# Two graph layers on one core: the segment softmax taken per chunk and clipped by carries, its key exchange brought forward, more value tiles, and other engines for three steps

## The chip, the cores and the metric

The kernel runs on one core of one Trainium2 chip. The metric is the device time of one execution in microseconds (us). Three runs of the kernel before gave 3033.27, 3036.22 and 3034.06 us, a median of 3034.06 us.

## The reference

A graph has 3125 nodes of 256 features and 50,000 edges sorted by destination. Layer one is three hops of weighted neighbour sums, each with two 256x256 products; layer two is one step of graph attention with 8 heads. Each is added to its input and layer-normalised.

```python
# layer 1, per hop
Hn = segment_sum(H[cols] * vals, rows) @ Wn[i].T + bn[i];  H = Hn + H @ Ws[i].T + bs[i];  H = elu(H) (not last)
# layer 2
alpha = <h_src, a_src> + <h_dst, a_dst> + sum(relu(edge_attr @ edge_W.T + edge_b) * h_dst)      # per edge and head
alpha = where(alpha >= 0, alpha, 0.2 * alpha)
ex = exp(alpha - segment_max(alpha, dst)[dst])
out = segment_sum(h_src * ex / segment_sum(ex, dst)[dst], dst) + bias
x = layernorm(x + out)
```

## The kernel before, in words

Edges are sorted on the chip and laid out as 416 chunks of 128, so that a chunk touches one window of 128 destination nodes (25 windows are used). All synchronisation is written by hand: each engine has its own program, and each operation that another must wait for raises a named semaphore. The order on every engine is the order of the code.

The stages, with their lines:

1. **Sort**, to about 556 us: GpSimd (POOL) scatters records by indirect DMA (L579, L589, L604).
2. **Adjacency blocks**, 570 to 1100 us: 90 steps of U = 8 blocks. For each block VectorE (DVE) or ScalarE (ACT) builds one-hots of the source (`rhot`), ACT weighs one-hots of the destination (`lw`, L1084), TensorE (PE) multiplies them into PSUM (L826), DVE merges the block with the one before of the same place (L1549), and SyncE (SP) stores it (128 KB, L484), to an address that it loads from a table once per step (L478). `RA` says how many of a step's 8 `rhot` tiles DVE makes in one instruction (L1538); the others ACT makes as a Square (L1090) and a Relu (L1093). A merge waits for the store of the same slot one step earlier.
3. **Hops**, to 2125 us, bound by PE's products (L896). At the end PE turns the node features back (L917), ACT copies them to `hcur` (L1135), and the keys of the chunks are transposed (L927) and copied by ACT (L1154). DVE marks the key breaks in `brk3` (L1660 to L1664).
4. **Score**, 2138 to 2658 us: POOL gathers the rows of the source nodes, 4 chunks per group, 104 groups (L618); SP stores each group for later (L524); PE, ACT and DVE look up the destination rows and form alpha. For each block of 16 chunks alpha is transposed into `alT` (a lane holds one chunk and head, 128 edges along the row), and DVE scans it forward and backward for the segment maximum inside the chunk (`scan_chunks`, L1700 and L1702).
5. **Carries**, 2658 to 2730 us: POOL adds the bias to all of `hcur` (L622). DVE writes the maxima of the chunk ends and their keys to `ends` (L1730, L1731); they go through DRAM to 8 lanes of 416 elements, where DVE scans over the chunks (L1735 to L1768), and back through DRAM as `cin`, the maximum that enters a chunk from the left and from the right (SP at L537, L540, L543 and L546). DVE scans all 26 blocks again with `cin` as start, forward (L1772) and backward (L1777), and subtracts (L1782). ACT takes the exponential (L1200), PE transposes back, ACT stores it to `s_sb` (L1203).
6. **Attend**, 2733 to 2982 us, in groups of 4 chunks: SP loads the kept rows (L528), POOL multiplies them by the exponentials into `val`, a ring of 2 tiles (L636); ACT builds one-hots (L1209, L1215) and copies the exponentials themselves into columns 256 to 263 of `val` (L1227), PE multiplies (L1013), DVE adds each chunk's result to its window (L1789). Which window that is, DVE reads from a table into registers, 8 values at a time, with a TENSOR_LOAD (L400).
7. **End**, 2982 to 3034 us: DVE divides by the sums (L1823), POOL adds to `hcur` (L650), DVE takes the statistics (L1828, L1840), the square root is ACT's (L1236), DVE normalises all 25 windows (L1849), SP stores them (L552, L555).

## Time and profile before

| what | us |
|---|---|
| median of three runs | 3034.06 |
| profiled execution, its own time | 3035.49 |
| its span, first to last instruction | 3033.7 |
| TensorE busy in it | 2438.7 (80%) |
| GpSimd busy | 1880.7 (62%) |
| VectorE busy | 1702.3 (56%) |
| ScalarE busy | 993.5 (33%) |

The profiled execution took 1.4 us longer than the median, and 1.8 us of its time lie around the span. Of the chain of work that ended last 54% is on PE, 12% on POOL and 7% on DVE, with 11% in which an engine waited for nothing that shows. The busy shares are means over the seven stages, which have different bounds. Engine names ending in q (DVEq, SPq) are an engine's sequencer: register work and the issuing of DMAs, which count as no busy time.

### The profile page before, as it was taken

How to read it: one execution, taken by the hardware profiler on the slowest of the kernel's cores; microseconds unless marked ns; L12 is line 12 of the kernel's file. 1: busy time of each engine (PE TensorE's matmuls, PEld its weight loads, DVE VectorE, ACT ScalarE, POOL GpSimd, SP SyncE). 2: the span in 40 equal slices, each digit the busy share in tenths (PEclk: the TensorE clock that was granted, in tenths of full speed). 3: DMA queues.
4: the chain of work that ended last, by engine and by line, in shares of the span. 5: the costliest groups of instructions: out<-in, count | busy, mean ns of one | idle time of the engine just before them, and what ended most of it. 6: DMA issues, size and time to landing. Idle time of an engine off the chain costs nothing.

```text
span 3033.7 us, 46185 instructions
## 1 busy us (share of the span) xinstructions
PE 2438.7 (80%) x9398; PEld 1579.2 (52%) x9399; DVE 1702.3 (56%) x4008; ACT 993.5 (33%) x2944; POOL 1880.7 (62%) x1739
## 2 busy tenths in 40 slices
PE   6999976477777679999899999999777767708882
PEld 5888843255555544445444454445555555506661
DVE  7765559899999940001344301113677666675557
ACT  1222221377777720000000000000433333318882
POOL 4777777787777870000067777760777777737774
PEclk9999999699999999999999999998888888859996
DMA  4000010355555555443344444452677777737772
GB/s 128 3 4 3 3 25 3 115 184 183 183 183 182 183 184 154 134 132 110 100 125 122 118 128 129 136 145 72 187 217 219 219 218 218 207 65 218 228 228 83
DMA packets 425353, 415.42 MB, mean 137 GB/s; under 512 B 85090, under 2 KB 411193, under 8 KB 424633
## 3 DMA queue, kind: packets, MB, share of 16 engines
q1 hardware_dynamic: 367385, 348.28, 36.8%
q0 software_dynamic: 57888, 66.23, 9.7%
q8 instruction: 32, 0.52, 0.1%
q14 instruction: 48, 0.39, 0.0%
HBM read 247.08 MB, written 167.17 MB: 137 GB/s over the span
## 4 chain that ended last, share of the span: by engine, by line
PE 54%; POOL 12%; issue 11%; DVE 7%; DVEq 4%; DMA 4%; ACT 3%; SPq 3%; ACTq 1%; POOLq 0%
PE psum L896 27%; POOL gath L618 7%; PE psum L826 5%; PE psum L708 5%; POOL rows_by_pair L579 5%; PE psum L693 3%; DVEq L400 2%; ACT lw L1084 2%; PE psum L888 2%; PE psum L968 2%; DMA gath<-gat_rows,rec 2%; SPq L484 2%; PE psum L1013 1%; PE psum L767 1%; PE psum L684 1%
## 5 line engine op out<-in xcount | busy, mean ns | idle before, releaser
L604 POOL DMA_INDIRECT rows_by_dst<-rec,place x392 | 381.6, 974 | 512.8 <-DVE place L1441 385.1
L896 PE MATMUL psum<-a_t,acc 128*128 128x512 f32 (+1 forms) x1400 | 553.7, 551 | 0.0
L589 POOL DMA_INDIRECT rows_by_low_digit<-rec,place x392 | 459.8, 1173 | 128.0 <-issue 128.0
L618 POOL DMA_INDIRECT gath<-gat_rows,rec x416 | 401.4, 965 | 214.1 <-issue 115.5
L826 PE MATMUL psum<-rhot,lw 128*128 128x256 f32 x1440 | 371.1, 414 | 169.7 <-ACT lw L1084 143.0
L579 POOL DMA_INDIRECT rows_by_pair<-rec,place x392 | 385.3, 983 | 161.9 <-issue 126.8
L826 PEld LDWEIGHTS psum<-rhot,lw 128*128 128x128 f32 x1440 | 281.9, 205 | 258.9 <-ACT lw L1084 182.2
L896 PEld LDWEIGHTS psum<-a_t,acc 128*128 128x128 f32 x1400 | 257.3, 195 | 272.1 <-issue 268.3
L1549 DVE SCALAR_TENSOR_TENSOR merged<-merged,same_of,psum 128x256 f32<-128x256 f32 x720 | 298.2, 476 | 19.1 <-PE psum L826 17.0
L896 PE MATMUL psum<-a_t,x 128*128 128x512 f32 (+1 forms) x700 | 294.4, 549 | 0.0
L1084 ACT ACTIVATE lw<-lhot,recs_pair 128x128 f32<-128x128 bf16 x720 | 228.5, 388 | 178.2 <-DVE lhot L1532 138.2
L968 PE MATMUL psum<-x,acc 128*128 x832 | 260.4, 461 | 4.6 <-DVE acc L1678 4.4
L1013 PE MATMUL psum<-ht 128*128 128x264 f32 x832 | 203.7, 397 | 45.7 <-DVE acc L1789 39.2
L636 POOL TENSOR_TENSOR ht<-gath,digits 128x1024 f32<-128x1024 f32 x104 | 197.2, 1913 | 54.5 <-PE psum L1013 48.5
L708 PEld LDWEIGHTS psum<-table,ohhiT 32*128 32x128 f32 x784 | 181.1, 318 | 53.5 <-issue 32.0
L968 PEld LDWEIGHTS psum<-x,acc 128*128 128x128 f32 x832 | 181.6, 233 | 51.5 <-issue 17.2
L1678 DVE TENSOR_TENSOR acc<-wT,psum 128x528 f32<-128x528 f32 x208 | 145.3, 698 | 104.8 <-PE psum L968 76.2
L1013 PEld LDWEIGHTS psum<-ht 128*128 128x128 f32 x832 | 154.1, 192 | 95.1 <-DVE acc L1789 59.7
L708 PE MATMUL psum<-table,ohhiT 32*128 32x16 f32 x784 | 202.2, 375 | 1.7 <-ACT table L1044 1.7
L1625 DVE TENSOR_SCALAR et<-et 128x512 f32<-128x512 f32 (+1 forms) x28 | 11.0, 394 | 335.1 <-ACT et L1112 334.6
L896 PEld LDWEIGHTS psum<-a_t,x 128*128 128x128 f32 x700 | 126.2, 191 | 114.0 <-issue 109.0
L1319 DVE SCALAR_TENSOR_TENSOR terms<-psum,kst,earlier 128x128 f32<-128x128 f32 (+1 forms) x392 | 139.9, 412 | 44.8 <-PE psum L693 34.3
(311 smaller groups left out, 3301.9 us busy)
## 6 DMA issues: line engine op xcount, KB each, us to landing
a_t<-adjacency SPq DMA_DIRECT2D x450, 256.0 KB, 2.7
adjacency<-merged SPq DMA_DIRECT2D x721, 128.0 KB
gat_h_by_edge<-gath SPq DMA_DIRECT2D x104, 528.0 KB, 4.1
gath<-gat_h_by_edge SPq DMA_DIRECT2D x104, 528.0 KB, 4.1
gath<-gat_rows,rec POOLq DMA_INDIRECT x416
rows_by_pair<-rec,place POOLq DMA_INDIRECT x392
rows_by_low_digit<-rec,place POOLq DMA_INDIRECT x392
rows_by_dst<-rec,place POOLq DMA_INDIRECT x392
```

The source lines that it names most:

```text
L579: pool.indirect_dma_start(out=rows_pair, in_=rec[:, c, :], out_offset=bass.IndirectOffsetOnAxis(ap=place[:, 0, c:c + 1], axis=0), in_offse ...
L589: pool.indirect_dma_start(out=rows_low, in_=rec[:, c, :], out_offset=bass.IndirectOffsetOnAxis(ap=place[:, 1, c:c + 1], axis=0), in_offset ...
L604: pool.indirect_dma_start(out=rows_dst, in_=rec[:, c, :], out_offset=bass.IndirectOffsetOnAxis(ap=place[:, 0, c:c + 1], axis=0), in_offset ...
L618: pool.indirect_dma_start(out=gath[:, g % 4, c % 4, :], out_offset=None, in_=hh_dram, in_offset=bass.IndirectOffsetOnAxis(ap=rec_i[:, c, 0 ...
L636: nc.gpsimd.tensor_tensor(val[:, q % 2, :, 0:D].rearrange("p c (h d) -> p c h d", h=HEADS), gath[:, q, :, 0:HX].rearrange("p c (h d) -> p ...
L708: pe.matmul(bank[7 * s][:, j * LO:(j + 1) * LO], ohhiT[:, 4 * s + j, :], table[:, half, :], start=True, stop=True, skip_group_check=True). ...
L826: pe.matmul(bank[j % 4][:, 0:SW], lw[:, p, j, :], rhot[:, p, j, :], start=True, stop=True).then_inc(s_bmm, 1)
L896: i = pe.matmul(sums[b], table_g[:, w, b * P:(b + 1) * P], a_t[:, q % NA, 0:width(g)], start=False, stop=w == USED - 1)
L968: i = pe.matmul(bank[4 + j][:, 0:HX], ohT[:, q % 2, j * P:(j + 1) * P], x0[:, bass.ds(ws[4 * (q % 2) + j], 1), :].rearrange("p c k -> p (c ...
L1013: pe.matmul(bank[4 * (q % 2) + j][:, 0:HX], onehot[:, q // 2, 4 * (q % 2) + j, :], val[:, q % 2, j, :], start=True, stop=True).then_inc(s_ ...
L1084: nc.scalar.activation(lw[:, p, j, :], lhot[:, p, j, :], ACT.Copy, scale=recs_pair[:, bass.ds(at, 1), 2]).then_inc(s_lw, 1)
L1549: v.scalar_tensor_tensor(out=merged[:, j, :], in0=merged[:, (j - 2) % U, :], scalar=same_of[:, bass.ds(s, 1)], in1=bank[j % 4][:, 0:SW], o ...
```

## The change

* `RA` is 5, so of a step's 8 `rhot` tiles DVE makes 5 and ACT 3.
* At the end of the hops the keys are transposed first; then the features are turned back, and DVE adds the bias as it stores them to `hcur`. ACT's copies and POOL's addition are gone.
* `scan_chunks` has nine operations per block instead of two: both scans; a scan each that marks with 0 the lanes of the chunk's last and first segment (others are very low); copies of the chunk's end maxima to `ends`; and three subtractions. After the carries have come, two clipping passes per block (`lower_first`, `lower_last`) replace scan, scan and subtraction.
* The keys of the chunk ends have a DRAM exchange of their own: stored when the breaks are marked, ahead of SP's first kept group, and read behind its last. Of the carry computation what depends on keys alone stands ahead of the wait for the end maxima. SP exchanges the maxima ahead of its loads of the first four kept groups.
* `val` is a ring of 4 tiles, and POOL, DVE and ACT wait for an earlier product. DVE copies the exponentials into it, two groups ahead, and ACT's copies are gone.
* The end is written out window by window in three parts (`FINAL`: windows 0 to 8, 9 to 17, 18 to 24). Statistics and root of a part are taken as soon as its windows are there. ACT normalises the first two parts and three windows of the last, DVE four. Five stores take the place of four.
* Semaphores are merged, which moves nothing.

```diff
-RA = 6
+RA = 5
+FINAL = [(0, 9, 9), (9, 18, 18), (18, USED, 21)]
+LOCAL = 9
...
-        val = ht_t[:, 0:8 * HX].rearrange("p (s c d) -> p s c d", s=2, c=4)
+        val = ht_t[:, 0:16 * HX].rearrange("p (s c d) -> p s c d", s=4, c=4)
...
+            sp.wait_ge(s_brk, 5)
+            sp.dma_start(edge_key_dram, end_keys[:, :, :].rearrange("p b k -> p (b k)")).then_inc(s_ends, 16)
+            sp.wait_ge(s_ends, 16)
             for g in range(NQ):
...
-            nc.gpsimd.tensor_tensor(hcur[:, :, :], hcur[:, :, :], bias_b[:, :].unsqueeze(1).broadcast_to([P, USED, D]),
-                                    ALU.add).then_inc(s_bias, 1)
...
-                    if not (first and q < 2):
-                        pool.wait_ge(s_mm, 4 * (g - 1))
+                    if not first:
+                        pool.wait_ge(s_mm, 4 * (g - 3))
...
-            for w in range(USED):
-                act.wait_ge(s_xb, w + 1)
-                nc.scalar.copy(hcur[:, w, :], bank[w % 4][:, 0:D]).then_inc(s_x1, 1)
...
-                    nc.scalar.copy(val[:, q % 2, :, D:HX], s_sb[:, bass.ds(4 * g, 4), :]).then_inc(s_vx, 1)
...
+            for w in range(USED):
+                dve.wait_ge(s_xb, w + 1)
+                v.tensor_tensor(hcur[:, w, :], bank[w % 4][:, 0:D], bias_b[:, :], ALU.add).then_inc(s_x1, 1)
...
             def scan_chunks(b):
...
+                v.tensor_tensor_scan(row, stop[:, 0:P], a, -BIG, ALU.add, ALU.max).then_inc(s_loc, 1)
+                v.tensor_tensor_scan(in_last[:, ::-1], stop[:, 1:P + 1][:, ::-1], low, 0.0, ALU.add, ALU.max).then_inc(s_loc, 1)
+                dve.wait_ge(s_loc, n + 1)
                 v.tensor_tensor_scan(back[:, ::-1], stop[:, 1:P + 1][:, ::-1], row[:, ::-1], -BIG, ALU.add,
-                                     ALU.max).then_inc(s_bw, 1)
+                                     ALU.max).then_inc(s_loc, 1)
+                dve.wait_ge(s_loc, n + 3)
+                v.tensor_tensor_scan(row, stop[:, 0:P], low, 0.0, ALU.add, ALU.max).then_inc(s_loc, 1)
+                v.tensor_copy(ends[:, b, 0:1], back[:, P - 1:P]).then_inc(s_loc, 1)
+                v.tensor_copy(ends[:, b, 1:2], back[:, 0:1]).then_inc(s_loc, 1)
+                dve.wait_ge(s_loc, n + 6)
+                v.tensor_tensor(back, a, back, ALU.subtract).then_inc(s_loc, 1)
+                v.tensor_tensor(row, a, row, ALU.subtract).then_inc(s_loc, 1)
+                dve.wait_ge(s_loc, n + 8)
+                v.tensor_tensor(a, a, in_last, ALU.subtract).then_inc(s_loc, 1)
...
+            def lower_first(b):
+                v.scalar_tensor_tensor(out=dotT[:, b, :], in0=sdeT[:, b, :], scalar=cin[:, b, 0:1], in1=dotT[:, b, :],
+                                       op0=ALU.subtract, op1=ALU.min).then_inc(s_first, 1)
...
+            def lower_last(b):
+                dve.wait_ge(s_first, b + 1)
+                v.scalar_tensor_tensor(out=alT[:, b, :], in0=alT[:, b, :], scalar=cin[:, b, 1:2], in1=dotT[:, b, :],
+                                       op0=ALU.subtract, op1=ALU.min).then_inc(s_mx, 1)
...
+            def exp_columns(g, q, first):
+                if not first:
+                    dve.wait_ge(s_mm, 4 * (g - 3))
+                v.tensor_copy(val[:, q, :, D:HX], s_sb[:, bass.ds(4 * g, 4), :]).then_inc(s_vx, 1)
```

Places at which the instructions move:

DVE in the score stage, the piece of a block of 16 chunks that `scan_chunks` writes (`ht` is the space of the scan results, `acc` that of the breaks, `digits` of `in_last`). Before:

```order
L1684 TENSOR_REDUCE ht<-acc 128x32
L1678 TENSOR_TENSOR acc<-wT,psum 128x528
L1700 SCALAR_TENSOR_TENSOR ht<-acc,alT 128x128
L1702 SCALAR_TENSOR_TENSOR ht<-acc,ht 128x128
L1670 TENSOR_SCALAR acc<-psum,lane_f 128x512
```

In the change:

```order
L1723 SCALAR_TENSOR_TENSOR ht<-acc,alT 128x128
L1724 SCALAR_TENSOR_TENSOR digits<-acc,low_c 128x128
L1726 SCALAR_TENSOR_TENSOR ht<-acc,ht 128x128
L1729 SCALAR_TENSOR_TENSOR ht<-acc,low_c 128x128
L1730 COPY ends<-ht 128x1
L1731 COPY ends<-ht 128x1
L1733 TENSOR_TENSOR ht<-alT,ht 128x128
L1734 TENSOR_TENSOR ht<-alT,ht 128x128
L1736 TENSOR_TENSOR alT<-alT,digits 128x128
```

Seven operations have come into each of the 26 blocks.

DVE in the attend loop, half a turn (8 chunks). Before (L400 loads the eight window numbers, ISA and REGISTER_ALU are register work):

```order
L400 REGISTER_ALU
L400 TENSOR_LOAD win_next
L1787 REGISTER_ALU
L1789 ISA
L1789 TENSOR_TENSOR acc<-acc,psum 128x264
L1785 REGISTER_ALU
L1789 ISA
L1789 TENSOR_TENSOR x<-x,psum 128x264
```

In the change, the start of the half turn:

```order
L1836 ISA
L1836 COPY ht<-digits 128x4x8
L405 ISA
L405 TENSOR_LOAD win_next
L1828 REGISTER_ALU
L1830 ISA
L1830 TENSOR_TENSOR acc<-acc,psum 128x264
```

And its middle, from the fourth addition to the fifth:

```order
L1830 TENSOR_TENSOR x<-x,psum 128x264
L1835 REGISTER_ALU
L1836 ISA
L1836 COPY ht<-digits 128x4x8
L1826 REGISTER_ALU
L1828 REGISTER_ALU
L1830 ISA
L1830 TENSOR_TENSOR acc<-acc,psum 128x264
```

One copy stands ahead of each TENSOR_LOAD, and one between the fourth and the fifth addition.

## Rows read from the trace of the kernel before

**Rows 1.** Busy time by stretch, score and attend stage: us, then each engine's busy us

```profile
2138.00:2658.00 520.00, 366.91 (x1799) 268.98 (x1798) 365.63 (x518) 173.15 (x545) 395.33 (x410) 0.85 0.75 214
2733.00:2982.00 249.00, 203.66 (x832) 154.07 (x832) 146.32 (x416) 213.40 (x617) 194.67 (x103) 0.99 0.74 217
```

**Rows 2.** SP in the adjacency stage: chain pieces (start, us, what); its table load

```profile
708.30 0.77 SPq L478
709.33 0.34 SPq L484
709.92 0.33 SPq L484
...
714.13 0.78 SPq L478
...
L478 SPq TENSOR_LOAD <-block_row x84: 700/766/814, 603.5 to 1087.0; - x84
```

**Rows 3.** Groups by line, 600 to 1090 us: busy us, mean ns, idle before

```profile
L1084 ACT ACTIVATE lw<-lhot,recs_pair 128x128 f32<-128x128 bf16 x673 | 213.6, 388 | 125.0 <-DVE lhot L1532 87.1 <-PE psum L826 37.9
L1538 DVE TENSOR_TENSOR rhot<-slo,iota_f 128x1536 f32<-128x1536 f32 x84 | 147.3, 1754 | 0.0
L1093 ACT ACTIVATE rhot<-apart,ones 128x256 f32<-128x256 f32 x169 | 85.9, 508 | 5.5
```

**Rows 4.** Groups by line, the score stage

```profile
L618 POOL DMA_INDIRECT gath<-gat_rows,rec x416 | 401.4, 965 | 214.1 <-issue 115.5 <-DMA gat_rows<-s_src 87.6 <-ACT digits L1187 11.0
```

**Rows 5.** Timeline of the carries: start, us, engine, line, tiles, idle before

```profile
2658.00 14.26 DVE L1702 TENSOR_TENSOR_SCAN ht<-acc,ht 128x128 f32<-128x128 f32 x1
2658.31 13.66 POOL L622 TENSOR_TENSOR hcur<-hcur,bias_b 128x6400 f32<-128x6400 f32 x1
...
2668.41 0.22 ACT L1187 COPY digits<-gath 128x32 f32<-128x32 f32 x1 [6.62 <-DMA gath<-gat_rows,rec]
...
2674.43 0.43 DVE L1702 TENSOR_TENSOR_SCAN ht<-acc,ht 128x128 f32<-128x128 f32 x1
...
2675.84 0.19 DVE L1730 COPY ends<-ht 128x26 f32<-128x26 f32 x1
2675.94 0.18 DVE L1731 COPY ends<-ht 128x26 f32<-128x26 f32 x1
...
2684.37 1.86 DVE L1735 COPY x<-x 8x416 f32<-8x416 f32 x4 [8.25 <-DMA x<-chunk_ends]
...
2691.90 1.01 DVE L1757 TENSOR_TENSOR_SCAN x<-x 8x416 f32<-8x416 f32 x1
...
2696.18 0.28 SPq L543 DMA_DIRECT2D chunk_carries<-x  x1
...
2699.77 9.88 DVE L1772 TENSOR_TENSOR_SCAN ht<-acc,cin,alT 128x128 f32<-128x128 f32 x26 [3.61 <-DMA cin<-chunk_carries]
...
2719.60 5.34 DVE L1782 TENSOR_TENSOR alT<-alT,ht 128x128 f32<-128x128 f32 x26
...
2730.51 3.78 POOL L636 TENSOR_TENSOR ht<-gath,digits 128x1024 f32<-128x1024 f32 x2 [5.07 <-ACT digits L1203]
```

**Rows 6.** Attend stage: DVE's table load (min/median/max ns); timeline

```profile
L400 DVEq TENSOR_LOAD <-win_next x49: 1841/1847/1864, 2747.3 to 2974.8; - x49
...
2965.62 0.42 DVE L1789 TENSOR_TENSOR x<-x,psum 128x264 f32 x1
...
2966.02 3.78 POOL L636 TENSOR_TENSOR ht<-gath,digits 128x1024 f32<-128x1024 f32 x2 [1.12 <-PE psum L1013]
...
2967.82 0.43 DVE L1789 TENSOR_TENSOR acc<-acc,psum 128x264 f32 x1 [1.77 <-PE psum L1013]
```

**Rows 7.** Timeline of the end

```profile
2992.06 21.62 POOL L650 TENSOR_TENSOR hcur<-hcur,acc  x25 [14.95 <-DVE acc L1823]
...
3016.82 8.17 DVE L1849 TENSOR_SCALAR hcur<-hcur,stat 128x256 f32<-128x256 f32 x25
...
3025.11 1.11 SPq L555 DMA_DIRECT2D out<-hcur  x1
```

More of the change, by code:

```diff
@@ L929, in _ @@
                 t.then_inc(s_kT, 1)
+            for w in range(USED):
+                if w >= 4:
+                    pe.wait_ge(s_x1, w - 3)
+                for b in range(2):
+                    i = pe.transpose(bank[w % 4][:, b * P:(b + 1) * P], ht[:, b, w * P:(w + 1) * P], identf[:, :])
+                i.then_inc(s_xb, 1)
+            pe.wait_ge(s_x1, USED)
             pe.wait_ge(s_kTs, len(quads))
@@ L1224, in attend @@
                         distances(g + 1, q + 1)
[L1225 to L1227 removed]
+                    if not first:
+                        act.wait_ge(s_mm, 4 * (g - 3))
                     onehots(g, q)
@@ L1234, in _ @@
             attend(NB - 1, False, True)
-            act.wait_ge(s_ln, 4)
-            nc.scalar.activation(stat[:, 0:USED, 2], stat[:, 0:USED, 1], ACT.Sqrt).then_inc(s_sq, 1)
+            for i, (w0, w1, on_act) in enumerate(FINAL):
+                act.wait_ge(s_ln, 3 + 3 * i)
+                nc.scalar.activation(stat[:, w0:w1, 2], stat[:, w0:w1, 1], ACT.Sqrt).then_inc(s_sq, 1)
+                act.wait_ge(s_ln, 5 + 3 * i)
+                for w in range(w0, on_act):
+                    nc.scalar.activation(hcur[:, w, :], hcur[:, w, :], ACT.Identity, bias=stat[:, w, 0:1],
+                                         scale=stat[:, w, 3:4]).then_inc(s_fin, 1)
         @block.vector
@@ L1774, in _ @@
[L1774 to L1782 removed]
+            dve.wait_ge(s_loc, LOCAL * NB)
@@ L1795, in sum_chunks @@
                     g = 4 * b + q
+                    if not (last and q >= 2):
+                        exp_columns(g + 2, (q + 2) % 4, first and q < 2)
                     if q % 2 == 0:
@@ new lines, in scales @@
+            def scales(i, w0, w1):
+                dve.wait_ge(s_sq, 2 * NG + 1 + i)
+                v.reciprocal(stat[:, w0:w1, 3], stat[:, w0:w1, 2]).then_inc(s_ln, 1)
+                dve.wait_ge(s_ln, 4 + 3 * i)
+                v.scalar_tensor_tensor(out=stat[:, w0:w1, 0], in0=stat[:, w0:w1, 0], scalar=-1.0, in1=stat[:, w0:w1, 3],
+                                       op0=ALU.mult, op1=ALU.mult).then_inc(s_ln, 1)
+            for w in range(USED + 3):
+                if w < USED:
+                    divide(w)
+                if w >= 3:
+                    stats(w - 3)
+                for i, (w0, w1, on_act) in enumerate(FINAL):
+                    if w - 3 == w1:
+                        scales(i, w0, w1)
+                    if w - 3 == w1 - 1:
+                        settle(i, w0, w1)
```

213 lines of the change are left out of this document (107 added, 106 removed).

## The prediction

> **What bounds the kernel now.** I read the chain of waits first, then busy time by stretch, then the timeline of each stretch that the change touches. In each, look for the engine that has no pause.
>
> *Adjacency, 530 us.* DVE looks like the bound, but SP is. Its stores leave 0.59 us apart, and with the table load a step of eight takes 714.13 - 708.30 = 5.83 us while it issues without a pause. Over the whole stage the same table load comes every (1087.0 - 603.5) / 83 = 5.825 us [rows 2]. The two agree, so SP never waits, and every merge in the end waits for a slot that SP frees.
>
> *Score, 520 us.* POOL issues a gather every 965 ns + 0.3 us: 416 of them are 517 us, and it waited 11.0 us in all for anyone downstream [rows 4]. DVE is busy 366 of the 520 us [rows 1].
>
> *Carries, 2658 to 2730.5.* One dependent line. At its head a DVE scan that takes 0.43 us elsewhere took 14.26, beside POOL's bias addition of 13.66; but the last gathered rows were copied at 2668.41, so most of that delay was hidden behind a DMA [rows 5].
>
> *Attend, 249 us.* PE is busy 204 us, ACT 213, POOL 195, DVE only 146 [rows 1], and yet DVE is the bound: after its eighth addition (2965.62) the next comes at 2967.82, because its sequencer spends 1.85 us in a TENSOR_LOAD, which comes every (2974.8 - 2747.3) / 48 = 4.74 us [rows 6]. 52 half turns of 4.74 are 246 us. Each instruction that DVE gets here lengthens the kernel; work taken off POOL, ACT or PE does not shorten it.
>
> *End.* POOL adds its last window at 2992.06 + 21.62 = 3013.68, DVE normalises from 3016.82 to 3024.99, the last store is issued at 3025.11 and the span ends at 3033.7, 8.6 us later, since all of the output is stored in these last microseconds [rows 7].
>
> **The change part by part.**
>
> *RA = 5: 0 us.* DVE's instruction falls from 1536 to 1280 columns: 1754 x 256 / 1536 = 0.29 us per step, 26 us over 90 steps if DVE were the bound. SP's 5.83 us stay, so I book nothing. ACT gets one Square and one Relu more per step, about 1.0 us by the Relu's 508 ns; its waits of 125.0 us over 84 steps, 1.5 each, cover that [rows 3]. Bounds: -26 us (SP not the bound after all) and 0.
>
> *Start of the score: 0 us.* 25 bias additions from PSUM replace ACT's copies and now stand between the key transposes and the breaks. They push DVE's first score work back by 1 or 2 us. POOL's gathers, which start before and set the stage's end, cover it; its fifth group needs the first kept row group stored, about 24 us after the first gather (16 x 1.26 = 20 us, with one held-up gather of 4), and SP's detour for the keys is two small transfers. Without that cover it would cost what it takes. Bounds 0 and 2.
>
> *Seven more DVE operations per block in the score: 0 us.* Two scans of 0.43 us, three subtractions of 5.34 / 26 = 0.21, two tiny copies 0.10 apart and three more waits on its own results: about 1.9 us per block, 46 us for the 24 that lie in the stage [rows 5]. DVE has 154 us free there [rows 1] and POOL waits for no one. Bounds 0 and 8, the latter if each burst held PE by a third of a microsecond.
>
> *Carries: -23 us.* The last copy still comes at 2668.6. Then alpha, 0.7, so 2669.4; two local passes of 2.8 us (four scans, two copies, three subtractions, three waits) end at 2674.9, with the last maximum stored by 2674.1. The exchange of the maxima no longer stands behind 2 MB of loads; priced like the store and load of the carries, 2699.77 - 2696.18 = 3.6, it is done at 2678, hidden behind DVE's work on the keys. That is 12 short operations and two copies of 1.86 / 4: the old line from 2684.37 to 2696.18 is 11.8, of which 0.9 (two copies), 2.0 (two scans), 1.3 (four operations) and 1.0 (two copies out) depend on maxima; some 6.0 are left, so 2680.9. Then those 5.2: 2686.1; the exchange, 3.6: 2689.7, against 2699.77. The passes over the blocks were 19.83 (two of scans) + 5.34. Now they are 52 clipping operations with a lane's scalar; between 0.21 (the subtraction) and 0.38 (the scan) [rows 5] I take 0.23, as they are elementwise: 12.0, ending at 2701.7. The tail from there to POOL's first product, 2730.51 - 2724.94 = 5.6, stays: 2707.3 against 2730.51, -23.2. Bounds of the clipping alone: 10.9 to 19.8 us, so -24 to -15. POOL's missing bias addition is inside this: it frees DVE at 2658.5, but the copy at 2668.6 is what DVE waits for next.
>
> *Attend: +20 us.* ACT's copies had slack; DVE's have none. The copy between the fourth and fifth addition and the one ahead of the TENSOR_LOAD lengthen the line by at least the 0.10 us at which two small copies follow one another, and at most by an addition's 0.34 ((4.74 - 1.85) / 8 = 0.36 with the loop) [rows 5, 6]. Each also needs register work. I take 0.18 each, nearer the lower end since they have 32 elements: 104 x 0.18 = 19, and 1 for waits on POOL (next). Bounds +10 and +37 from this alone. The ring of four gains nothing: POOL's 1.91 us per group fits twice into 4.74.
>
> A DVE operation on SBUF can be held by POOL for POOL's whole instruction, as the 14.26 us show [rows 5]. In the loop POOL's two multiplications start just as DVE's eight additions end (2966.02 after 2965.62) and run 3.78 us, to 2969.80 [rows 6]; the first addition of the next half turn is at 2967.82, so the middle copy would ask at 2969.2 and wait 0.6 in the old rhythm. In the slower one it asks 0.36 later and waits 0.2 or less; each wait shifts the phase so that the next is shorter. The copy ahead of the TENSOR_LOAD may wait for a whole multiplication, 1.9 us, but the load runs beside it and hides that. The Trainium skill ("SBUF — State Buffer", Who interferes with whom) says that a copy in a 2-port mode and a GpSimd instruction take the shared pair exclusively, and the later one blocks for the whole instruction. Without the phase argument the rule would give the second rival below.
>
> *End: -9 us.* The windows are still paced by POOL and DVE in turn, 21.62 / 25 = 0.86 us. Two interposed settlements of about 1.1 push the last window to 3015.9; the last settlement has 7 windows, some 2.0 us against 3.1; four normalisations of 8.17 / 25 = 0.33 end at 3019.3 against 3024.99. Two thirds of the output left earlier, so the last store needs some 5 us instead of 8.6: end 3025 against 3033.7 [rows 7]. Bounds -12 (both gains larger, no settlements in the way) and -5 (only the normalising).
>
> **Sum**: 0 + 0 + 0 - 23 + 20 - 9 = -12. The profiled execution would take 3035.5 - 12 = 3023.5, the median, 1.4 lower, 3022.
>
> **Rivals.**
>
> *The copies cost an addition's pitch each* (+37 in place of +20, with -32 elsewhere): 3039. In part, +31: 3033. For it: a dependent register chain as long as an addition's stands before each. Against: small copies start 0.10 apart. This is the case of no change.
>
> *The copies are held by POOL.* If the phase does not settle, the middle copy meets a multiplication four times in five and waits half of 1.91: 52 x 0.76 = 40 us more, so 3062; if the held copy also keeps the TENSOR_LOAD from starting, or POOL's second multiplication goes ahead of it, as much again, 3100. For it: POOL is busy 195 of 249 us, and the 14.26 us. Against: the phase above. It decides against the kernel once the two copies of a half turn cost over 32 / 52 = 0.62 us together.
>
> *DVE bounds the adjacency stage* (RA does what a look at busy shares says): -26 more, 2996. Against: SP's two equal periods.
>
> *The local passes stretch the score stage*, 8 us: 3030, by DVE holding PE in each block. Against: 154 us free.
>
> **How the numbers follow.** About 0.2%, 6 us, is what a measurement of this kernel can tell from no change. The forecast's case (3008 to 3030) 0.55, the copies at a full pitch 0.17, held by POOL 0.18, DVE as the bound 0.05, the stretched score 0.05. Faster than 3028 are the fifth, nearly all of the first: 0.05 + 0.51, and a third of the last: 0.58. Within 6 us: 0.17. Slower: 0.25. The range leaves out the DVE-bound case and the upper part of the POOL case: 3004 to 3055. The likeliest case alone is 3008 to 3030.
>
> **What would show it.** Stores of a step still 5.83 us apart; carries, from the last copy of gathered rows to POOL's first product, 39 us instead of 62; DVE's table load every 5.1 us or so instead of 4.74, with the copies 0.1 to 0.3 us long; the clipping passes 12 us; 43 us instead of 52 from the last addition to the end. Copies over a microsecond long would show POOL's hold, a step under 5.7 us that SP was not the bound, and gathers with pauses over 0.3 us that the score stage was hit. A table load still at 4.74 would prove me wrong on attend, and the kernel would then take some 3002.

## The result, and the profile after

| | before | changed |
|---|---|---|
| median of 20 runs, us | 3035.52 | 3029.99 |
| span of the profiled execution, us | 3033.7 | 3028.5 |

The ratio is 0.9983 (95% interval 0.9976 to 0.9989): 5.5 us faster (3 to 7 by the interval), where 12 were forecast. Direction and range held, the size did not. The spans differ by 5.2 us, and the sum of the prediction can be put beside that term by term. All boundaries are rows of this section and of [rows 5 to 7].

| term | forecast, us | by the two traces, us |
|---|---|---|
| adjacency (`RA`) | 0 | 0 |
| score, its start and the seven operations | 0 | 2669.87 - 2668.41 = +1.5 |
| carries: last gathered copy to GpSimd's first product | -23 | 39.43 - 62.10 = -22.7 |
| attend: to the long addition behind it | +20 | 274.34 - 251.70 = +22.6 |
| end | -9 | 44.86 - 51.49 = -6.6 |
| sum | -12 | -5.2 |

The long addition (L1864) follows the last addition of attend; before, the same instruction was L1813, at 2982.21.

```profile
2982.21 7.31 DVE L1813 TENSOR_TENSOR acc<-acc,x 128x6864 f32<-128x6864 f32 x1
```

**Adjacency.** Line groups of the changed kernel, 600 to 1090 us, and SyncE's table load (min/median/max ns, first and last start) [rows 2, 3]:

```profile
L1099 ACT ACTIVATE lw<-lhot,recs_pair 128x128 f32<-128x128 bf16 x674 | 221.9, 387 | 44.7 <-DVE lhot L1548 33.1 <-PE psum L842 10.2
...
L483 SPq TENSOR_LOAD <-block_row x85: 676/760/797, 599.3 to 1087.5; - x85
```

ScalarE's waits ahead of L1099 fell from 125.0 us to 44.7, and nothing came of it, for better or worse: a step is (1087.5 - 599.3) / 84 = 5.81 us against 5.83.

**Score.** GpSimd's gathers of the changed kernel and of the kernel before, 2138 us to their last; then the start of the stage in the changed kernel:

```profile
L636 POOL DMA_INDIRECT gath<-gat_rows,rec x410 | 397.5, 970 | 125.0 <-issue 114.7 <-ACT digits L1198 10.4
```

```profile
L618 POOL DMA_INDIRECT gath<-gat_rows,rec x410 | 395.7, 965 | 125.0 <-issue 114.0 <-ACT digits L1187 11.0
```

```profile
2140.13 3.59 DVE L1679 TENSOR_TENSOR acc<-alT 128x3302 f32<-128x3302 f32 x1
...
2140.43 5.54 POOL L636 DMA_INDIRECT gath<-gat_rows,rec  x1 [0.31 <-issue]
...
2143.94 1.91 DVE L1683 TENSOR_SCALAR acc<-acc 128x3354 f32<-128x3354 f32 x1
```

The first gather starts when it did before (2130.32 against 2130.37), and GpSimd waits no longer than before, but its gathers themselves take 1.8 us more. One is held beside VectorE's work on the breaks, for 5.54 us (5.14 before). Of the others 24 take 0.98 to 1.14 us, where 8 did before, and each of these runs beside VectorE operations of a block; that these are the cause was not tested.

**Carries.** Timeline, as in [rows 5]:

```profile
2669.87 0.22 ACT L1198 COPY digits<-gath 128x32 f32<-128x32 f32 x1 [6.39 <-DMA gath<-gat_rows,rec]
...
2670.19 0.29 DVE L1710 TENSOR_TENSOR digits<-digits,ht 128x128 f32<-128x128 f32 x1 [7.22 <-ACT digits L1198]
...
2681.52 0.51 DVE L1790 COPY x<-x 8x416 f32<-8x416 f32 x1
...
2689.92 0.88 DVE L1810 SCALAR_TENSOR_TENSOR ht<-ht,cin 128x128 f32<-128x128 f32 x3 [3.71 <-DMA cin<-chunk_carries]
...
2702.78 0.87 DVE L1815 SCALAR_TENSOR_TENSOR alT<-alT,cin,ht 128x128 f32<-128x128 f32 x3
...
2709.30 3.80 POOL L652 TENSOR_TENSOR ht<-gath,digits 128x1024 f32<-128x1024 f32 x2 [7.78 <-ACT digits L1214]
```

The maxima (L1790) are taken up without a wait right behind the key work. The carries are back at 2689.92, against 2699.77. The clipping takes 2703.65 - 2689.92 = 13.7 us.

One part of the gain is easily missed. VectorE's first operation on the last copied rows now starts 2670.19 - 2669.87 = 0.32 us behind the copy. Before, it was 2673.44 - 2668.41 = 5.03 us, because the scan held beside GpSimd's bias addition ended only at 2672.26 [rows 5] and a reduction stood behind it:

```profile
2673.44 0.29 DVE L1691 TENSOR_TENSOR digits<-digits,ht 128x128 f32<-128x128 f32 x1
```

**Attend.** VectorE's table loads in the 24 turns of the loop; its copies over the stage; and one half turn:

```profile
L405 DVEq TENSOR_LOAD <-win_next x49: 1841/1844/1870, 2722.9 to 2972.0; - x49
```

```profile
L1836 DVE COPY ht<-digits 128x32 f32 (+1 forms) x104 | 97.2, 937 | 9.8 <-ACT digits L1214 5.6 <-PE psum L1028 4.2
```

```profile
2962.08 1.66 DVE L1836 COPY ht<-digits 128x32 f32 x1 [0.18 <-PE psum L1028]
...
2964.27 0.43 DVE L1830 TENSOR_TENSOR acc<-acc,psum 128x264 f32 x1 [0.53 <-issue]
...
2965.30 0.42 DVE L1830 TENSOR_TENSOR x<-x,psum 128x264 f32 x1
2965.64 0.17 DVE L1836 COPY ht<-digits 128x32 f32 x1
2965.93 0.43 DVE L1830 TENSOR_TENSOR acc<-acc,psum 128x264 f32 x1
...
2966.96 0.42 DVE L1830 TENSOR_TENSOR x<-x,psum 128x264 f32 x1
2967.10 3.79 POOL L652 TENSOR_TENSOR ht<-gath,digits 128x1024 f32<-128x1024 f32 x2 [1.52 <-PE psum L1028]
2967.30 1.75 DVE L1836 COPY ht<-digits 128x32 f32 x1
...
2969.37 0.43 DVE L1830 TENSOR_TENSOR acc<-acc,psum 128x264 f32 x1 [0.32 <-issue]
```

The load comes every (2972.0 - 2722.9) / 48 = 5.19 us instead of 4.74. (Half turns differ by turns, since every second one closes the loop: 4.57 and 4.92 us before, 5.09 and 5.28 now.) The copy ahead of the load, 1.75 us long, ends with GpSimd's first multiplication (2967.10 + 1.91); without its hold it is the 0.17 us of the one in the middle. The load beside it starts at 2967.29, 0.01 us ahead of the copy. Of the 48 middle copies in the loop 47 take 0.17 or 0.18 us, of the 48 ahead of a load 46 take 1.63 to 1.75. The mean of 937 ns is a mean of these two kinds and describes neither.

**End.** Timeline of the changed kernel [rows 7]:

```profile
2983.64 7.31 DVE L1864 TENSOR_TENSOR acc<-acc,x 128x6864 f32<-128x6864 f32 x1
...
3013.32 4.53 ACT L1250 ACTIVATE hcur<-hcur,stat 128x256 f32<-128x256 f32 x9 [1.11 <-DVE stat L1893]
...
3013.88 2.55 POOL L666 TENSOR_TENSOR hcur<-hcur,acc  x3 [0.62 <-DVE acc L1873]
...
3018.44 1.58 ACT L1250 ACTIVATE hcur<-hcur,stat 128x256 f32<-128x256 f32 x3 [0.48 <-DVE stat L1893]
```

SyncE's stores in a shorter stretch of the same timeline, and what the DMA engines moved from 3005 to 3029 us, in 40 slices of 0.6 us:

```profile
3017.88 3.85 SPq L571 DMA_DIRECT2D out<-hcur  x3
3021.77 1.09 SPq L573 DMA_DIRECT2D out<-hcur  x1
```

```profile
GB/s 0 0 0 0 0 0 0 179 348 345 348 350 346 50 0 0 0 0 0 0 0 0 2 326 350 345 343 335 353 329 350 343 205 3 14 24 24 22 0 0
```

The last window is normalised at 3020.02 and the span ends 8.5 us later. The first part of the output left in the first burst. The second part is normalised only at 3013.32 + 4.53 = 3017.85, and its 1.18 MB leave in one burst with the 0.8 MB behind it, at some 345 GB/s from 3018.8 to 3025. Then comes a thin end: 14, 24, 24 and 22 GB/s over 0.6 us each are some 50 KB, about the 54 KB of the 53 rows of window 24, which have a store of their own (L573). The kernel before has the same thin end, so it is a part of its 8.6 us too; no run was made without it.

### The profile page after: what moved, and what is told of

It reads as the page before. It is cut to its first block, busy times and chain, and to the rows that moved or that the text cites. A ratio compares the mean times of both kernels' runs of the same rounds, so it can differ in the third digit from the quotient of the medians.

```text
span 3028.5 us, 46970 instructions
## 1 busy us (share of the span) xinstructions
PE 2444.8 (81%) x9398; PEld 1573.7 (52%) x9399; DVE 1797.2 (59%) x4277; ACT 1068.3 (35%) x3018; POOL 1846.8 (61%) x1738
## 4 chain that ended last, share of the span: by engine, by line
PE 50%; POOL 14%; issue 11%; SPq 8%; DVE 6%; DMA 4%; DVEq 3%; ACT 2%; ACTq 0%; POOLq 0%
PE psum L912 27%; POOL gath L636 9%; SPq L489 6%; PE psum L724 5%; POOL rows_by_pair L597 5%; PE psum L1028 4%; DVEq L405 3%; PE psum L709 3%; PE psum L904 2%; DMA gath<-gat_rows,rec 2%; PE psum L783 1%; PE psum L842 1%; SPq L483 1%; PE psum L700 1%; ACT lw L1099 1%
## 5 line engine op out<-in xcount | busy, mean ns | idle before, releaser
L607 POOL DMA_INDIRECT rows_by_low_digit<-rec,place x392 | 438.0, 1117 | 127.6 <-issue 127.6
L842 PE MATMUL psum<-rhot,lw 128*128 128x256 f32 x1440 | 381.2, 419 | 160.1 <-ACT lw L1099 126.5
L1565 DVE SCALAR_TENSOR_TENSOR merged<-merged,same_of,psum 128x256 f32<-128x256 f32 x720 | 310.0, 477 | 30.5 <-PE psum L842 18.7
L1099 ACT ACTIVATE lw<-lhot,recs_pair 128x128 f32<-128x128 bf16 x720 | 236.8, 387 | 94.8 <-DVE lhot L1548 83.0
```

The source lines that it names most:

```text
L607: pool.indirect_dma_start(out=rows_low, in_=rec[:, c, :], out_offset=bass.IndirectOffsetOnAxis(ap=place[:, 1, c:c + 1], axis=0), in_offset ...
L842: pe.matmul(bank[j % 4][:, 0:SW], lw[:, p, j, :], rhot[:, p, j, :], start=True, stop=True).then_inc(s_bmm, 1)
L1099: nc.scalar.activation(lw[:, p, j, :], lhot[:, p, j, :], ACT.Copy, scale=recs_pair[:, bass.ds(at, 1), 2]).then_inc(s_lw, 1)
L1565: v.scalar_tensor_tensor(out=merged[:, j, :], in0=merged[:, (j - 2) % U, :], scalar=same_of[:, bass.ds(s, 1)], in1=bank[j % 4][:, 0:SW], o ...
```

## The experiments

The 18 runs went to two kinds of chip. On one the kernel before took 3036 to 3038 us, as in the result. On the other, the slower chip below, every kernel took 4210 to 4340 us, because waits between engines are longer there in the sort, adjacency and score stages. The ratios there are uncertain by 0.2%, some 9 us. The changed kernel itself gave 1.0024 (1.0006 to 1.0041) on it: it is slower than the kernel before there, not faster, and why was not traced. I compare runs of one kind, and read stages from rows; attend takes nearly the same time on both (274.35 us and 273.45 us for the changed kernel).

> The changed kernel itself, on the chip of this group of runs, as the mark that the others are held against. 5.5 us below the kernel before on a chip like the first; on the chip of the first and third group, where both take 4260 us, the same difference within its uncertainty.

VectorE's load comes every (4196.3 - 3947.2) / 48 = 5.19 us again.

**1. The copies back on ScalarE.**

```diff
+                    nc.scalar.copy(val[:, q, :, D:HX], s_sb[:, bass.ds(4 * g, 4), :]).then_inc(s_vx, 1)
                     onehots(g, q)
...
-                    if not (last and q >= 2):
-                        exp_columns(g + 2, (q + 2) % 4, first and q < 2)
```

> The changed kernel, with the copies of the exponentials given back to ScalarE; the ring of four value tiles stays. Theory A: the copies on VectorE are the whole of what attend has lost, through the register work that its sequencer has for each, and the ring is worth nothing. Then attend takes 22.7 us less, VectorE's table load comes every 4.74 us again, and the kernel takes 3030.0 - 22.7 = 3007. Rival B: the longer attend stage comes from the ring or the later waits of GpSimd; it then keeps its length, and the time stays at 3030. Rival C: ScalarE with its copies is now the bound, and only part comes back: 3015 to 3025.

0.9968 (0.9954 to 0.9981) where the changed kernel has 1.0024 on this kind of chip: 0.56%, about 24 us less, with some 9 us of uncertainty. The load of VectorE comes every (4179.6 - 3947.9) / 48 = 4.83 us, 52 x 0.36 = 19 us:

```profile
L405 DVEq TENSOR_LOAD <-win_next x49: 1841/1848/1868, 3947.9 to 4179.6; - x49
```

Theory A. The ring of four is worth nothing, and ScalarE is not the bound. The same attend code stands in three kernels below. In `best3` the load comes every 4.83 us again, in `best2` and `best2_2`, one on each kind of chip, every 4.74 us, the old pace. `best2` and `best3` differ only by an edit to an earlier stage, the pieces of experiment 8. So 0.09 us per half turn, 4 to 5 us in all, come and go with code outside the loop; the cause was not tested.

**2. Is it the number of copies?** One copy of 64 elements in the middle of each half turn instead of two of 32.

```diff
-                v.tensor_copy(val[:, q, :, D:HX], s_sb[:, bass.ds(4 * g, 4), :]).then_inc(s_vx, 1)
+                v.tensor_copy(val[:, q:q + 2, :, D:HX],
+                              s_sb[:, bass.ds(4 * g, 8), :].rearrange("p (s c) h -> p s c h", s=2)).then_inc(s_vx, 2)
...
+                    if q % 2 == 1 and not (last and q == 3):
+                        exp_columns(g + 1, (q + 1) % 4, first and q < 2)
```

> The changed kernel with one copy of the exponentials per two groups (128x64 in place of two of 128x32), in the middle of VectorE's half turn; the copy ahead of the table load is gone. Theory A (register work for each copy): about half of the loss comes back, 52 x 0.22 = 11 us, so 3019, with a table load every 4.97 us. Rival B: the middle copy is the one that costs, because GpSimd holds it: nothing comes back or it gets longer, 3030 or more, and copies in the middle last over 1 us.

0.9997 (0.9982 to 1.0012). The load comes every 5.11 us, only 0.08 less than 5.19. Two half turns in a row:

```profile
4132.75 3.78 POOL L652 TENSOR_TENSOR ht<-gath,digits 128x1024 f32<-128x1024 f32 x2 [1.65 <-PE psum L1028]
...
4136.10 0.48 DVE L1836 COPY ht<-digits 128x64 f32 x1
...
4141.52 0.18 DVE L1836 COPY ht<-digits 128x64 f32 x1
```

Every second copy lasts 0.48 us and ends with GpSimd's second multiplication (4136.53). Half turns last 4.81 and 5.41 us by turns, where the kernel before had 4.57 and 4.92. So neither theory alone: an unheld copy costs about 0.24 us of register work and pitch, one held by GpSimd 0.5 us, and the new rhythm brings such a one every second time.

**3. Is the held copy really free because the load runs beside it?** The load ahead of the copy.

```diff
+                    if q % 2 == 0:
+                        ws = windows(...)
                     if not (last and q >= 2):
                         exp_columns(g + 2, (q + 2) % 4, first and q < 2)
-                    if q % 2 == 0:
-                        ws = windows(...)
```

> The changed kernel with VectorE's table load ahead of the copy of the exponentials instead of behind it, so that nothing runs beside a copy that GpSimd holds. Theory A: the copies of 1.7 us ahead of the load are held for the rest of a GpSimd multiplication and are free only because the load of 1.84 us runs beside them; behind the load such a copy stands in the line of additions, and each half turn gets longer by whatever GpSimd's two multiplications (3.78 us, begun as the eighth addition ends) have left when the load is through: up to 1.9 us, 52 times, +60 to +100 us, or less where the phase shifts. Rival B: the phase settles so that a copy meets no multiplication, and the order does not matter: 3030 within 5 us.

1.0178 (1.0161 to 1.0196), 0.0154 above the changed kernel on its kind of chip, 66 us by the times, with some 10 us of uncertainty, and 52 x (6.65 - 5.19) = 76 us by the loads, which come every 6.65 us:

```profile
L405 DVEq TENSOR_LOAD <-win_next x49: 1841/1845/1861, 3959.5 to 4278.9; - x49
```

```profile
4179.80 1.91 POOL L652 TENSOR_TENSOR ht<-gath,digits 128x1024 f32<-128x1024 f32 x1 [4.60 <-PE psum L1028]
...
4179.94 1.80 DVE L1836 COPY ht<-digits 128x32 f32 x1 [1.70 <-PE psum L1028]
...
4182.68 3.79 POOL L652 TENSOR_TENSOR ht<-gath,digits 128x1024 f32<-128x1024 f32 x2 [0.97 <-PE psum L1028]
4183.02 1.62 DVE L1836 COPY ht<-digits 128x32 f32 x1
4184.55 0.42 DVE L1830 TENSOR_TENSOR acc<-acc,psum 128x264 f32 x1
```

Theory A. The copy at 4179.94 stands behind its load, and 46 of 48 such copies are held for 1 to 1.8 us, now in the line of additions. Of the middle ones 33 stay at 0.17 us and 11 are held for 1.4 to 1.65 us, as the one at 4183.02. So most middle copies are spared here too, and what costs most is the held copy with nothing beside it. This hold was a rival of the prediction, one exchange of two lines away.

**4. Do waits of the sequencer pace the additions?** The copies are on ScalarE as in experiment 1, and VectorE waits for TensorE once per four additions.

```diff
             def add(n, k, w):
-                dve.wait_ge(s_mm, n + 1)
+                if k % 4 == 0:
+                    dve.wait_ge(s_mm, n + 4)
```

> The changed kernel with the copies of the exponentials on ScalarE and, in attend, one wait of VectorE on TensorE's products per four additions instead of one per addition. Theory A: VectorE's sequencer paces attend, since each addition stands 0.34 us behind the one before while register work and two waits go by; with three waits in four gone, an addition follows in about 0.28, so 416 x 0.05 = some 20 us more than the 20 us that the copies alone give: 3030 - 40 = 2990. Rival B: the additions themselves pace it (264 elements): their pitch stays 0.34, and only the 20 us of the copies come, 3010. Rival C: the later first addition of a group costs as much as the waits gave: table load every 4.8 us or more.

3011.99 us, 0.9916 (0.9902 to 0.9929): against 0.9983 that is 20 us less, what the copies give. The load comes every (2953.1 - 2722.5) / 48 = 4.80 us, and additions still start 0.34 us apart:

```profile
2864.83 0.42 DVE L1832 TENSOR_TENSOR acc<-acc,psum 128x264 f32 x1
2865.17 0.43 DVE L1832 TENSOR_TENSOR x<-x,psum 128x264 f32 x1
```

Rival B: three waits fewer in four change nothing inside a row of additions. Rival C had 4.8 us or more as its mark, and the first addition does start later behind the load, 2.16 us against 2.09; but with all its waits the loop took 4.83 and 4.74 us (experiment 1), so the mark tells nothing. What costs is the break in the row.

**5. What bounds the adjacency stage?** `RA` back to 6; addresses of 16 stores by one load; both; and the 16 addresses on top of experiment 4 (`best`).

```diff
-            with sp.Fori(0, STEPS) as t:
+            with sp.Fori(0, STEPS // 2) as t2:
...
-                    block_row[0:1, bass.ds(t * U, U)], ...
+                    block_row[0:1, bass.ds(t2 * 2 * U, 2 * U)], ...
```

> The changed kernel with RA = 6 again. Theory A: SyncE bounds the adjacency stage, so this edit of the change was worth nothing: a step of 5.81 us, 3030 within 1.5 us. Rival B: VectorE bounds it: 90 x 0.29 = +26 us, 3056. Between: a part of it, +3 to +10.

> The changed kernel, with SyncE loading the addresses of 16 stores at once in the adjacency stage, every second step, instead of 8 in every step. Theory A: SyncE's issuing is the bound of this stage. A load of 0.77 us falls away in every second step; if the longer load costs less than 0.8 us more, a step takes some 5.5 us in place of 5.81, where VectorE (0.36 us without work per step now) becomes the bound: 90 x 0.3 = -27 us, 3003; at least -10 us. Rival B: the stores themselves, or VectorE, bound the stage: no change, 3030.

> The changed kernel with addresses for 16 stores at once and RA = 6. Theory A: without SyncE as the bound RA counts: VectorE's 0.29 us more per step take back what its 0.36 us of idle time does not cover; the step is 5.6 to 5.75 us, later than in the run with RA = 5 by 0 to 0.15 us. Rival B: VectorE never bounds it, the step is the same as with RA = 5 and 16 addresses.

> As the run before, and SyncE's addresses for 16 stores at once in the adjacency stage. Theory A (SyncE bounds that stage): the table load of 16 costs about 1.2 us in place of 2 x 0.75, 0.15 to 0.2 us per step, and with one load and one loop turn fewer in two steps 90 x 0.2 = 18 us, until VectorE bounds it: step 5.6 us in place of 5.81, and some 18 us below the run before. Rival B: no difference to the run before.

| run | RA | addresses a load | step, us | ratio to before | changed kernel on such a chip |
|---|---|---|---|---|---|
| ra6 | 6 | 8 | 5.80 | 1.0012 (0.9994 to 1.0030) | 1.0024 |
| sp16 | 5 | 16 | 5.45 | 0.9935 (0.9915 to 0.9954) | 1.0024 |
| sp16_ra6 | 6 | 16 | 5.72 | 0.9943 (0.9929 to 0.9956) | 0.9983 |
| best | 5 | 16 | 5.47 | 0.9820 (0.9807 to 0.9834) | 0.9983 |

The steps are from rows like this one of `best`, (1058.2 - 609.3) / 82 = 5.47, and for `ra6` (1814.1 - 1315.2) / 86 = 5.80:

```profile
L483 SPq TENSOR_LOAD <-block_row x42: 1230/1240/1255, 609.3 to 1058.2; - x42
```

```profile
L483 SPq TENSOR_LOAD <-block_row x87: 506/748/773, 1315.2 to 1814.1; - x87
```

Theory A in all four: `ra6` has the step of the changed kernel on the same kind of chip, (1813.5 - 1314.5) / 86 = 5.80 us in `after_again`. SyncE bounds the stage, and `RA` is worth nothing while it does. With SyncE relieved, RA = 5 instead of 6 is worth (5.72 - 5.47) x 90 = 22 us, nearly the 26 that VectorE's shorter instruction gives, and the kernel drops from 3011.99 to 2982.62 us, 29 us where I had expected 18: one load of 1.24 us and one loop turn in place of two of each saves more than the loads alone. VectorE is then nearly without a pause, busy 431 of 445 us (610 to 1055 us, `best`). TensorE's granted clock rose too, from 0.93 in that stretch of `act_one_wait` to 1.00 in `best`, but stayed at 0.93 in `sp16_ra6`. TensorE is busy only 308 of the 445 us, so I put the 22 us down to VectorE; no run separates the two.

**6. The order of SyncE's transfers in the carries.** The loads of the first four kept groups ahead of the exchange of the maxima.

```diff
+            for g in range(4):
+                load_kept(g)
             sp.wait_ge(s_loc, LOCAL * NB - 3)
             sp.dma_start(edge_dram, ...)
...
-            for g in range(4):
-                load_kept(g)
             sp.wait_ge(s_line, 17)
```

> The changed kernel with SyncE's loads of the first four kept groups ahead of the exchange of the end maxima, as before the change. Theory A: the maxima then stand behind 2 MB of loads and come 8.25 us after their last value is stored instead of being there when VectorE asks; VectorE's key work hides 5.9 us of it, so about 2 to 3 us are lost, +2.5 us. Rival B: the order of these transfers was the main gain: +7 us or more. Rival C: nothing, since the loads have started 5 us earlier and are nearly through.

3034.24 us, 0.9990 (0.9981 to 0.9999). VectorE waits 2.79 us for the maxima, and from the last gathered copy (2671.48) to the first clipping it takes 22.70 us instead of 2689.92 - 2669.87 = 20.05, 2.65 more, as theory A has it:

```profile
2677.59 0.62 SPq L548 DMA_DIRECT2D chunk_ends<-ends  x1
...
2683.81 0.29 SPq L550 DMA_DIRECT2D x<-chunk_ends  x1
2685.89 0.51 DVE L1790 COPY x<-x 8x416 f32<-8x416 f32 x1 [2.79 <-DMA x<-chunk_ends]
```

Of the 22.7 us of the carries this order is 2.65. By the rows the clipping in place of three passes is (19.83 + 5.34) - 13.73 = 11.4 us, and the missing bias addition of GpSimd 5.03 - 0.32 = 4.7. The rest is the key work taken out of the line, less the longer local passes. No run takes these apart.

**7. The end of the kernel before, in the changed kernel.** One settlement, all 25 normalisations on VectorE, stores of 8 windows, in VectorE's loop over the windows.

```diff
-            for w in range(USED + 3):
-                if w < USED:
-                    divide(w)
-                if w >= 3:
-                    stats(w - 3)
...
+            with dve.Fori(3, USED) as w:
+                divide(w)
+                stats(w - 3)
```

> The changed kernel with the end as it was before the change: one settlement of all windows, VectorE normalises all 25, stores in groups of 8 windows. Theory A: the end of the change is worth what the two traces differ by behind the last addition, 51.5 - 44.9 = 6.6 us: 3036.6 where the changed kernel takes 3030. Rival B: more, the 9 us of my forecast, and something else in the changed kernel took 2.4 back: 3039.

> The changed kernel with the end of the kernel before, once more, beside the changed kernel on the same chip. Theory A: 6.6 us more than the changed kernel, and 51.5 us from the last long addition to the end as in the kernel before. Rival B: 9 us or more.

> The end of the kernel before in the changed kernel, for a chip like the one of the first result (about 3035 us). Theory A: the ratio to the kernel before rises from 0.9983 to 1.0004 (6.6 us), and from the last long addition to the end it takes 51.5 us. Rival B: 9 us, 1.0012.

1.0041 (1.0025 to 1.0056) and 1.0051 (1.0038 to 1.0064) beside 1.0024 on the slower chip, and 3041.32 us, 1.0016 (1.0007 to 1.0025) beside 0.9983 on the other: 7 and 12 us more than the changed kernel there, and 10 us here. The trace of the last one takes 3039.5 - 2985.18 = 54.3 us from the long addition on, 2.8 more than the kernel before with the same code. Line groups of the stretch from division to statistics, here and in the kernel before:

```profile
L1860 DVE TENSOR_TENSOR acc<-acc,s_src (+1 forms) x25 | 14.4, 584 | 3.0 <-issue 2.8
```

```profile
L1823 DVE TENSOR_TENSOR acc<-acc,s_src (+1 forms) x25 | 10.9, 446 | 1.5
```

```profile
3000.13 0.95 DVE L1860 TENSOR_TENSOR acc<-acc,s_src  x1 [0.26 <-issue]
```

Every third division is held for 0.5 us beside GpSimd's addition, so 25 windows take 24.5 us instead of 21.6, and the two runs on the slower chip show the same 54.4 us. A turn of the loop takes 0.90, 1.04 and 1.19 us by turns, where the kernel before has 0.88 throughout. The loop stands at another place in the program; that this brings the other rhythm was not tested. So the end of the change is worth 6.6 us against the kernel before and 9.4 (54.3 - 44.9) against the same end in its own program; theory A and rival B each had one of the two. Nothing in the changed kernel took 2.4 us back, as rival B has it; the old end itself is slower in this program.

**8. The held gather.** The two long operations on the breaks in 26 pieces each.

```diff
-            v.tensor_tensor(brk3[:, :, 1:P], K[:, :, 1:P], K[:, :, 0:P - 1], ALU.not_equal).then_inc(s_brk, 1)
+            for b in range(NB):
+                ins = v.tensor_tensor(brk3[:, b, 1:P], K[:, b, 1:P], K[:, b, 0:P - 1], ALU.not_equal)
+            ins.then_inc(s_brk, 1)
```

> The changed kernel with each of the two long operations on the key breaks at the start of the score stage (3.59 and 1.91 us) written as 26 short ones. Theory A: one gather of GpSimd is held for 5.54 us in place of 0.95 because it does not get its turn at SBUF beside long VectorE operations; short ones let it through, and the stage, which GpSimd bounds, ends up to 4.5 us earlier: 3025.5. Rival B: it is held as long as VectorE works in SBUF without a pause, in pieces or not, and since the pieces take longer (52 x 0.21 = 10.9 us against 5.5) the hold grows: 3030 to 3035.

> Short operations on the key breaks once more, for a chip on which GpSimd bounds the score stage (in the first run of this kernel it waited for others and the question did not arise). Theory A: no gather is held for long, and the stage ends up to 4.5 us earlier: 4.5 us less than the changed kernel. Rival B: the hold lasts as long as VectorE works in SBUF, 9 us here: 0 to 4 us more than the changed kernel.

1.0032 (1.0019 to 1.0044) and 1.0013 (0.9998 to 1.0027) beside 1.0024: the times tell nothing. In `split_breaks` GpSimd stood waiting for others while the pieces ran, but not in `split_breaks_2`. There one gather passed in 0.95 us, and the next was held for 4.74 us, pieces or no pieces:

```profile
3225.69 5.35 DVE L1680 TENSOR_TENSOR acc<-alT 128x127 f32<-128x127 f32 x26
...
3227.17 4.74 POOL L636 DMA_INDIRECT gath<-gat_rows,rec  x1 [0.30 <-issue]
```

The last run has the pieces too, on the faster chip:

**9. All together.** Copies on ScalarE, 16 addresses, and the last part of the output in two stores; `best2` and `best2_2` also have the pieces of experiment 8, `best3` does not.

```diff
+            sp.wait_ge(s_fin_v, 4)
+            sp.dma_start(out[FULLW * P:N, :], hcur[0:N - FULLW * P, FULLW, :]).then_inc(s_out, 16)
+            sp.wait_ge(s_fin, 21)
+            sp.dma_start(nodes(out[18 * P:FULLW * P, :]), hcur[:, 18:FULLW, :]).then_inc(s_out, 16)
```

> Copies of the exponentials on ScalarE, addresses of 16 stores at once, the key breaks in short operations, and the last part of the output in two stores instead of three (windows 18 to 23 as one, behind the 53 rows of window 24). Theory A: 2983 as the run with the first two, less 4.5 for the breaks, less 1.1 for a store issue that no longer stands behind the last normalisation: 2977. Rival B: the breaks give nothing or cost some 2 us: 2982 to 2985.

> Copies of the exponentials on ScalarE, addresses of 16 stores at once, and the last part of the output in two stores instead of three; the key breaks as in the changed kernel. The earlier run with the first two and fewer waits took 2983 us, 1.8% less than the kernel before. Theory A: the merged store gives 1.1 us and the waits gave nothing: 2982, ratio 0.9815. Rival B: the larger last store (6 windows, 768 KB) takes as long to drain as it saves in issue: no difference, 0.982.

> All edits together (copies on ScalarE, 16 addresses at once, short break operations, merged last store), for a chip like the one of the first result. Theory A: no gather is held for 5 us, the score stage ends 4.5 us earlier, and the kernel takes 2977. Rival B: the hold is as long or longer in pieces, 2982 to 2986.

0.9900 (0.9885 to 0.9916) and 0.9909 (0.9888 to 0.9930) on the slower chip; 2980.51 us, 0.9820 (0.9807 to 0.9834), on the other. The start of its score stage:

```profile
2108.02 5.30 DVE L1674 TENSOR_TENSOR acc<-alT 128x127 f32<-128x127 f32 x26
...
2111.05 3.13 POOL L629 DMA_INDIRECT gath<-gat_rows,rec  x1 [0.30 <-issue]
...
2113.56 4.11 DVE L1680 TENSOR_SCALAR acc<-acc 128x129 f32<-128x129 f32 x26
...
2126.58 0.95 POOL L629 DMA_INDIRECT gath<-gat_rows,rec  x1 [6.10 <-ACT digits L1191]
```

Two gathers pass in 0.96 and 1.09 us, then one is held for 3.13. In both runs the held gather ends 0.9 us behind the last piece of the comparison (2113.32 and 3231.04), so the comparison holds a gather in pieces as well, after one or two have passed. Beside the pieces of L1680 gathers pass in 0.95 us. But the last piece ends 9.65 us after the first begins, against 5.72 in the changed kernel, everything downstream starts later, and GpSimd then stands 6.10 us at its fifth group. From first to last gather it takes 533.6 us, against 528.6 in `best`. Neither theory, and a loss of 5 us in this stage. Against `best` attend gives back 3.0 us of it (251.6 us against 254.6, the two rhythms of experiment 1), and the gathers start 2.9 us earlier, which was not traced; so the two kernels have one ratio, 0.9820. The merged store brought 0.4 us (44.4 us from the long addition to the end against 44.9), nearer B than A: the burst of data and its thin end set the time, not the issues. `best3`, without the pieces, was not run on the faster chip. By the gather times it would save 5 us there, and by its attend, 4 us longer than that of `best2` (255.4 us against 251.1), lose nearly all of it.

## Why the prediction came out as it did

What failed is the size of the sum, and two terms are most of it: the price of the copies in attend, and the last store of the end. Term by term:

**"RA = 5: 0 us": right,** and shown both ways (experiment 5). The two equal periods of SyncE in the trace of before had pointed to it; busy shares pointed at VectorE.

**"Start of the score: 0 us" and "Seven more DVE operations per block: 0 us": together 1.5 us, inside their bounds.** The step said that GpSimd "waits for no one". It did not wait, but its gathers got slower, 397.5 us for 410 against 395.7: 0.4 from the hold at the start (5.54 against 5.14), the rest in the 24 gathers, 8 before, that take a little longer beside VectorE's operations. (Its 517 us for the gathers are 401.4 busy and 115.5 of issue; 416 times 0.965 + 0.3 would be 526, and first to last they took 528.) A free engine's busy time is no cover for an operation that slows the bound itself.

**"Carries: -23": mechanism right, and the size (-22.7) partly by luck.** The carries came back at 2689.92 (forecast 2689.7), but the last copy was 1.3 us later than assumed: from it to the carries the line took 20.05 us, where the sum has 21.1. (In that sum the key work should have been 11.8 - 5.2 = 6.6 us, not 6.0; it took 5.84.) The clipping was under-sized, 0.264 us for each instead of 0.23, 13.7 us instead of 12.0. Together 39.4 us to GpSimd's first product against 39. The tail was as forecast, 5.6.

**"Attend: +20": mechanism right, 22.6.** The bound and the phase argument held: middle copies stay unheld, the copy ahead of the load is held for 1.75 us and costs nothing for it. The price of each copy was mis-sized, 0.22 to 0.23 us, not 0.18: 0.45 per half turn. In microseconds this is the largest miss. In the middle, additions that stood 0.34 us apart stand 0.43 and 0.63 us apart by turns (2965.30 to 2965.93); the rest is the copy's register work ahead of the load, which starts 0.33 us behind the last addition instead of 0.10 (in a half turn that does not close the loop). With the Trainium skill's rule ("SBUF — State Buffer", Who interferes with whom), by which the later of the two is blocked until the other's instruction is through, the trace agrees: the copy of 2967.30 ends at 2969.05, GpSimd's first multiplication at 2969.01. Whether the copy runs in a 2-port mode, which that rule is about, the trace does not show. What the hold costs was decided by what stood behind the copy: nothing in the change, some 70 us in experiment 3.

**"End: -9": the step whose reasoning failed, -6.6.** "Two thirds of the output left earlier, so the last store needs some 5 us instead of 8.6" was wrong: only one third had left. ScalarE has the second part ready only 2.2 us before the third, and from the last normalisation to the end it took 8.5 us, the 8.6 of before. That cost 3.5 us against the "some 5". The other half was right: settlement 2.01 us (2.0), and the last window at 3016.43, 0.9 us earlier than the forecast 3015.9 with the later start of 1.4 would have it. The 9.4 us of experiment 7 do not make the -9 right: they are against an end that lost 2.8 us of its own.

The four misses, 1.5, 0.3, 2.6 and 2.4 us, are each small, and all have one sign. For the start of the score, the seven operations, the clipping and the copies I took the price at or near the low end of its range, and for the end I counted on an early store that did not happen. Against a sum of -12 made of -32 and +20, that was enough to halve it.

## What to carry to other kernels

An engine that paces a stage pays for an instruction that breaks its row of equal ones, however short: here a copy of 0.17 us cost 0.23 in the line, and it belonged on an engine with slack. Before tuning how work is shared between two engines, look whether a third, a queue here, sets the period: `RA` was worth 0, and 22 us once SyncE issued faster. When terms of both signs nearly cancel, the error of the sum is that of the large terms, so a forecast of a small difference needs the whole range of each price, costs and gains alike.

## What the runs showed that I had not expected

- One short operation's place decides over some 70 us: 52 copies behind a table load instead of ahead of it (experiment 3).
- A table load of 8 values costs SyncE 0.76 us and VectorE 1.84. For 16 SyncE needs 1.19 to 1.24.
- The same end of the program took 51.5 us in one kernel and 54.3, three times, in another (experiment 7).
- The same attend loop took 4.74 us per half turn in some kernels and 4.83 in others, with an edit in an earlier stage as the only difference (experiment 1).
- Two VectorE operations on the breaks, of 3.59 and 1.91 us, held a gather of GpSimd until both were through. In 26 pieces each, 0.2 us apart, the comparison still held one to its end, after one or two had passed, and the other held none (experiments 8 and 9).
